# The products with v of two attention steps taken together in a two-layer transformer kernel

## What is computed

```
x = x + attention(layernorm(x))
x = x + ffn(layernorm(x))
attention: p = softmax(causal(q k^T / 4 [+ alibi in layer 0])); o = p v; o Wo
ffn:       down(silu(gate(x)) * up(x))
```

## Time and profile before

| | |
|---|---|
| median of 3 runs | 487.1 us (485.09 to 487.35) |
| profiled execution | 488.24 us, its span 486.4 us |
| TensorE busy | 445.6 us (92%) |
| VectorE busy | 315.8 us (65%) |
| ScalarE busy | 229.7 us (47%) |
| products with v, L622 | 768 records, 81.9 us busy |
| attention of layer 0 | from the first scores at 55.3 us to the last product at 177 us |
| attention of layer 1 | from 300.4 us to 425 us |

### The profile page before, as it was taken

One profiled execution on the slowest core, in us unless ns is written; L12 is line 12 of the kernel. 1 busy time (PEld: TensorE's weight loads), 2 busy tenths in 40 slices (PEclk: granted clock), 3 DMA queues, 4 the chain that ended last, 5 costly groups with the idle time before them and its releaser, 6 DMA issues.

```text
span 486.4 us, 7518 instructions
## 1 busy us (share of the span) xinstructions
PE 445.6 (92%) x2904; PEld 228.8 (47%) x2904; DVE 315.8 (65%) x624; ACT 229.7 (47%) x360; POOL 102.5 (21%) x85
## 2 busy tenths in 40 slices
PE   1899799999999989999999896999999998997997
PEld 1357444434334247434575362544343433374466
DVE  4555789997977029322235577889988782087883
ACT  4454544565666753311002531444566566724960
POOL 4543000000000001195951067000000000011680
PEclk9999999999999999999999996899999999998999
DMA  8999600000000000102001962200000000000002
GB/s 233 151 196 244 172 11 1 1 2 3 0 3 1 3 5 1 65 2 65 0 0 57 224 174 64 70 2 1 2 1 1 2 1 2 0 2 0 2 12 76
DMA packets 23895, 22.52 MB, mean 46 GB/s; under 512 B 5194, under 2 KB 23114, under 8 KB 23850
## 3 DMA queue, kind: packets, MB, share of 16 engines
q1 hardware_dynamic: 22132, 19.02, 17.6%
q0 software_dynamic: 608, 2.50, 1.7%
q10 hardware_dynamic: 1120, 0.53, 0.4%
HBM read 8.27 MB, written 1.05 MB: 19 GB/s over the span
## 4 chain that ended last, share of the span: by engine, by line
PE 75%; DVE 12%; DMA 4%; ACT 4%; issue 3%; SPq 1%; POOL 0%; DVEq 0%; ACTq 0%
PE ps L622 14%; PE ps L593 13%; PE ps L607 12%; PE ps L705 9%; PE ps L744 6%; PE ps L720 5%; DVE mx L958 5%; PE ps L710 4%; PE ps L728 3%; PE ps L610 3%; PE ps L596 2%; DMA oT<-in_L_attn_Wo 2%; ACT prob L856 2%; PE ps L534 1%; DVE stats L924 1%
## 5 line engine op out<-in xcount | busy, mean ns | idle before, releaser
L958 DVE TENSOR_REDUCE mx<-ps 128x1 f32<-128x512 f32 (+3 forms) x304 | 185.4, 656 | 39.3 <-PE ps L596 28.2
L856 ACT ACTIVATE prob<-ps 128x1024 f32<-128x1024 f32 (+1 forms) x192 | 146.7, 809 | 98.8 <-PE ps L610 75.4
L593 PE MATMUL ps<-kS,qS 99*128 99x512 bf16 (+7 forms) x384 | 111.1, 336 | 4.8 <-DVE mx L958 2.8
L607 PE MATMUL ps<-qS,kS 101*128 101x512 bf16 (+7 forms) x384 | 100.1, 330 | 3.9 <-DMA qS<-mT 2.1
L622 PE MATMUL ps<-prob,v 128*32 128x512 f32 (+3 forms) x768 | 81.9, 498 | 0.0
L593 PEld LDWEIGHTS ps<-kS,qS 99*128 99x128 bf16 (+1 forms) x384 | 35.8, 99 | 76.7 <-DVE mx L958 55.2
L452 POOL TENSOR_SCALAR ve<-mv 128x4 f32<-128x4 f32 x8 | 1.8, 229 | 309.5 <-DVE mv L926 309.5
L607 PEld LDWEIGHTS ps<-qS,kS 101*128 101x128 bf16 (+1 forms) x384 | 35.9, 98 | 42.0 <-ACT prob L856 19.1
L610 PE MATMUL ps<-mask_k,identb 128*128 128x128 bf16 x256 | 50.3, 221 | 0.0
L596 PE MATMUL ps<-mask_q,identb 128*128 128x128 bf16 x256 | 50.2, 226 | 0.0
L705 PE MATMUL ps<-xnT,gu0T 128*128 128x512 f32 (+1 forms) x96 | 42.2, 596 | 0.7 <-ACT xnT L783 0.7
(11 more groups left out here) (117 smaller groups left out, 499.1 us busy)
## 6 DMA issues: line engine op xcount, KB each, us to landing
qS<-parts SPq DMA_DIRECT2D x24, 128.0 KB, 5.0
kS<-parts SPq DMA_DIRECT2D x24, 128.0 KB, 4.2
qS<-prob SPq DMA_DIRECT2D x12, 128.0 KB, 3.8
kS<-prob SPq DMA_DIRECT2D x12, 128.0 KB, 3.5
qS<-xn SPq DMA_DIRECT2D x12, 128.0 KB, 2.4
kS<-xn SPq DMA_DIRECT2D x12, 128.0 KB, 2.4
x<-in_L_attn_x SPq DMA_DIRECT2D x2, 512.0 KB, 5.6
out<-x SPq DMA_DIRECT2D x8, 128.0 KB, 1.7
```

Of the source, the lines that this page charges most:

```text
L593: mmi = nc.tensor.matmul(span, qS[0:K_MAX[L], c, g * G + h, qt * P:(qt + 1) * P], kS[0:K_MAX[L], g * G + h, key0:key0 + keys], start=True, ...
L607: mmi = nc.tensor.matmul(bank[:, off:CH], kS[0:K_EXP[L], h, kt * P:(kt + 1) * P], qS[0:K_EXP[L], c, h, off:CH], start=True, stop=not diagonal)
L856: nc.scalar.activation(prob[:, n % 3, 2 * pair:2 * pair + 2, off:CH], ps[:, 2 * (m % 2):2 * (m % 2) + 2, off:CH], ACT.Exp, scale=SCALE).th ...
L958: ins = nc.vector.tensor_reduce(mx[:, slot, qt, heads[0]:heads[-1] + 1, part], src, AX_X, ALU.max)
```

## The change

The products of two successive steps are done together, behind the scores of the step that follows them: at each even step s from 2 on, those of steps s-2 and s-1; at the end those of 46 and 47 as before.

```diff
--- before.py
+++ after.py
@@ -134,7 +134,6 @@
 V_FIRST = 5
 W1_AFTER = 4
 FIRST_MAX_BEFORE = 6
-PV_LAG = 1
 
 
 def attention_order():
@@ -184,12 +183,11 @@
         upto(pace(at + 0.25 * wide(s)))
         order.append(("exp", s, 1))
         upto(pace(at + 0.5 * wide(s)))
-        if s >= PV_LAG:
-            order.append(("pv", s - PV_LAG))
+        if s >= 2 and s % 2 == 0:
+            order += [("pv", s - 2), ("pv", s - 1)]
         at += wide(s)
     upto(len(entries))
-    for s in range(len(exp_steps()) - PV_LAG, len(exp_steps())):
-        order.append(("pv", s))
+    order += [("pv", len(exp_steps()) - 2), ("pv", len(exp_steps()) - 1)]
     return order
```

## The result

The changed kernel took 497.2 us (median of 4, 495.2 to 497.9) against 487.2 us for the one before (median of 4, 485.1 to 489.0) on the same chip. The ratio is 1.020, with a 95% interval of 1.015 to 1.025: slower, by 7 to 12 us. The forecast was 496.9 us in a range of 493 to 502.

The account below looks back on a forecast made before the run. TensorE was taken to set the pace, with little room for bursts beside VectorE (83%) and ScalarE (77%). Waits of +8.3 less 3.5 us for switches a layer, +9.8 in both, on 487.1 gave 496.9 us, range 493 to 502.

Parts of the forecast that it names:

- Switches removed (-6.9 us): TensorE in attention: 19 fewer blocks a layer at 0.18 us each, 3.5 us a layer, 6.9 us saved in both.
- Waits on VectorE (first two stretches): TensorE's maxima wait for banks: per layer +2.1 us in steps 0 to 15, +3.4 in steps 16 to 37.
- The rival by which VectorE would keep up in the maxima, and only the tail pay (485.7 us): Attention: VectorE keeps up, ScalarE doesn't; -5.6 + 4.2 = -1.4 us, no change; chance 0.05.
- Waits on ScalarE (tail): Steps 38 to 47: scores wait for exponentials to free banks; TensorE's waits 1.6 to 4.4 us, +2.8 a layer.
- The first wait of a pair of steps of full width: Tail: after two products, the second step's first scores wait 0.89 us for ScalarE.
- The junction: Between two products back to back on TensorE: costs nothing beyond a half's spacing, 0.46 us.
- The second bound of that unknown, a junction that costs a switch: Between paired products: 0.18 us at 23 places a layer, up to +8.3 us; 500 to 505 us, chance 0.09.
- The sum: Both layers' attention: waits +8.3 less switches 3.5, +4.8 to +4.9 us a layer, +9.8 us in both.
- The clock: Tails of both layers: new waits make TensorE's granted clock fall once in each; about 505 us, chance 0.02.

Follow-up runs that it names:

- the first experiment: Against the kernel before the change: products in pairs only up to step 38, single in the tail; 492.0 us, ratio 1.011.
- the spread orders: Against the kernel before, maxima placed by a table for free VectorE banks: single products 480.9 us (0.983); pairs up to step 38 478.5 us (0.981).

## Why the prediction was right

The mechanism held: both engines' pauses, in both stretches, at nearly the size that was laid out. The agreement of the total, 496.9 forecast and 497.2 measured, is closer than the terms deserve. They come to about +8 us, not +9.8: the new junctions between products, put at nothing, gave back 2.2 us.

**Switches removed (-6.9 us).** The spacings of 0.15 in (175.53 to 175.68, for one) and 0.54 out stand unchanged around the new blocks, and there are 24 blocks of 16 records a layer. (The forecast's parts by stretch leave out the block at the end, which is the same in both orders; the 19 that fall away are right.) The step held.

**Waits on VectorE (first two stretches).** Read from the starts in the changed kernel's timeline, each start's distance beyond its form's own, TensorE waits 5.3 us in steps 0 to 15 and 4.75 in steps 16 to 37 of layer 0. The forecast was 5.5 and 4.7. The first experiment shows them alone, at somewhat under half of the loss, and the spread orders show their cause: VectorE's load is the same, only the places differ, and the time goes away. The rival by which VectorE would keep up in the maxima, and only the tail pay (485.7 us), falls with the first experiment.

**Waits on ScalarE (tail).** 4.7 us against a forecast 4.4. In layer 0 the first exponential of step 43 starts 0.28 us later than its scores would let it. The old kernel's starts equally late (at 168.78, behind scores sent from 167.80 on), and I have no explanation for it; there it cost nothing, for from step 38's first scores to the last product both layers take 18.4 us. Layer 1's tail of the changed kernel is without it, and 0.28 us shorter. The first wait of a pair of steps of full width was to be 0.89; it is 1.18 with that delay and 0.91 in layer 1.

**The junction.** This is the one term that was missed, and on the side of less. The halves of the second product start earlier than I took them to. The timeline of the changed kernel, cut behind the first product of the pair at 170.20:

```profile
171.08 0.61 PE L620 MATMUL ps<-prob,v 128*32 128x512 f32 x4
```

That is 0.88 us behind the first, not 0.91, and the next scores follow 0.97 later, not 1.00. A pair takes 0.05 us less than two products laid end to end, at 23 new junctions a layer, 2.2 us in both. The second bound of that unknown, a junction that costs a switch, falls with it; I had taken the lower end, and the truth lay a little under it. In layer 0 the waits grew by 8.5 us, 0.2 more than forecast. A shorter block gives the other engines less of a pause, which may be a part of it; no run separates that.

**The sum.** In layer 0 TensorE waits 14.8 us (the three figures above) against 6.3. Twice that difference is 17.0, less 0.3 for layer 1's shorter tail; less 6.9 for switches and 2.2 for junctions it is 7.6 us. The forecast had 9.8. The profiled executions differ by 9.0 (497.22 and 488.24). Where, the timelines say: layer 1's first scores and last two products before, and layer 0's last two, layer 1's first scores and its last two products after (the earlier trace rows has layer 0's before, and 55.34 is its first scores after):

```profile
300.39 0.58 PE L607 MATMUL ps<-qS,kS 98*128 98x512 bf16 x1 [0.19 <-issue]
423.90 1.07 PE L622 MATMUL ps<-prob,v 128*32 128x256 f32 x16
```

```profile
182.47 1.07 PE L620 MATMUL ps<-prob,v 128*32 128x256 f32 x16
306.39 0.58 PE L605 MATMUL ps<-qS,kS 98*128 98x512 bf16 x1 [0.21 <-issue]
433.71 1.07 PE L620 MATMUL ps<-prob,v 128*32 128x256 f32 x16
```

Layer 1's attention grew by 3.8 us (123.51 to 127.32) and layer 0's by 5.9 (121.24 to 127.13), against 4.9 forecast for each. Of the 5.9 the clock made 1.5, so the orders account for 4.4 + 3.8 = 8.2 us. The terms come to 0.6 us less, 0.3 a layer; waits read from the starts are no more exact than that. That the medians differ by 10.0 is within the spread of single runs, some 3 to 4 us, and within the measured interval, as 8.2 is. So it is partly luck that the forecast fits to 0.3 us: the orders account for 1.6 us less than it had.

**The clock.** Its rival was to cost several microseconds in the tails, where the granted clock stayed at 1.00. But in the changed kernel's profiled execution it fell at the beginning of layer 0's attention, directly behind the 2.1 us wait for the first scores, to 0.50 (1.2 GHz instead of 2.4), and was back at full at 59 us:

```profile
54.00:58.00 4.00, 2.66 (x13) 1.60 (x14) 1.04 (x2) 1.02 (x1) 0.00 (x0) 0.70 0.74 204
56.00:58.00 2.00, 2.00 (x11) 1.29 (x10) 0.69 (x1) 1.02 (x1) 0.00 (x0) 0.50 0.73 206
```

and before, with the same wait, it didn't:

```profile
54.00:58.00 4.00, 2.68 (x26) 1.84 (x26) 1.71 (x4) 1.93 (x2) 0.00 (x0) 1.00 0.74 203
```

The first experiment prices the fall. Up to step 38 its order is that of the changed kernel, and it had no fall there. From the first scores to those of step 16 it takes 44.5 us, and the changed kernel 46.0:

```profile
53.80:98.30 44.50, 41.44 (x381) 21.95 (x382) 37.86 (x74) 21.26 (x32) 0.00 (x0) 1.00 0.12 31
```

```profile
55.30:101.30 46.00, 42.87 (x381) 22.92 (x382) 37.97 (x74) 21.37 (x32) 0.00 (x0) 0.96 0.10 28
```

The execution of before has a fall elsewhere, behind layer 1's attention:

```profile
442.00:447.00 5.00, 3.65 (x12) 1.65 (x13) 2.58 (x8) 1.82 (x3) 1.24 (x2) 0.66 0.00 0
```

From layer 1's last two products to the end it takes 0.8 us longer than the changed kernel. So although the mean granted clock is 0.986 in both, the clock is some 0.7 of the 9.0 us between the two profiles. I had taken the row of before as evidence that a wait of 2.1 us leaves the clock alone; it shows only that it did once.

## What to carry to other kernels

In this kernel an engine that is 99% busy was not the only bound, for its neighbours stood at 77 to 86% behind two or three buffers: what it saves by bunching one kind of work it can lose by sending the other kind in bursts. Before work is grouped on the busiest engine, count what its pauses were used for by those that empty its buffers, and lay out one period by start times. The places of the interleaved work were worth more here (1.7 to 1.9%) than the switches that the grouping saved (6.9 us, 1.4%).

## What had not been expected of the hardware

A second product directly behind the first starts and runs a little faster than the first. The products are float32, on 32 columns of the array, and each has two halves of four records. From the start of a half to the start of the next it takes 0.45 us inside the first product of a pair (170.20 to 170.65), 0.43 from there to the second product (171.08), and 0.43 inside the second. In single products, too, a first half takes 0.45 (127.34 to 127.80).

And the granted clock fell to half behind a wait of 2.1 us in one execution and not in another with the same instructions up to there.
